# Attention scores as a 64-row and a 32-row product, queries copied earlier and moved once a period

## The chip, the cores and the metric

The kernel runs on one core of one Trainium2 chip. The metric is device time in microseconds (us) of one execution; the kernel before takes 558.39 us, the median of 3 runs (557.83 to 560.25). TensorE multiplies matrices (PE in the profile, its weight loads PEld), VectorE is DVE, ScalarE is ACT, GpSimd is POOL, and SyncE (SP) issues most of the DMAs.

## The reference

One layer in four parts, on x of 16 sequences, 128 steps, 128 features:

```
h   = LSTM(x, h0 = cond)                      # 128 steps in sequence
lat = h @ Wkv_down                            # 32 latents per position
k,v = lat @ Wk_up, lat @ Wv_up                # 16 heads of 64
y   = causal_softmax(q k^T / 8) v @ Wout,  q = h @ Wq
x1  = x + y
g   = GRU(x1, h0 = cond), every 4th state also through tanh(g @ Wp + bp)
out = x1 + sum over the 2 best of 8 experts: gate_e * (gelu(g @ w1_e + b1_e) @ w2_e + b2_e)
```

The kernel folds Wq and Wk_up into one matrix, so that a score is a product over 32 latents: score(head, t, s) = q'(head, t) · lat(s), with q' of 32 numbers for each head and position. Most values are carried as a high and a low part in 16-bit floats; a product of two such values is formed as high·high + high·low + low·high.

## The kernel before

The whole kernel is one pipeline of 154 steps, written out by hand: for each step k every engine has a fixed list of instructions, and semaphores order them across engines. In step k TensorE does step k of the LSTM (pL) and step k - 18 of the GRU (pG; LAG = 18); between the two recurrences the rest of the work is laid as filler. Engines issue in order, so an instruction that waits holds back everything behind it on its engine.

The rest goes in periods of 8 steps. At k = 8, 16, ... `lat_q` computes the latents (pY) and the queries q' (pC) of the last 8 positions of all 16 sequences. The queries lie in pC as 128 rows (4 heads of 32 latents) by 512 columns (4 groups of heads, 8 positions, 16 sequences). `q_copy` (ACT, in the same step) takes their high part into `qh`, `q_rest` (DVE, a step later) the low part. `spread_queries` (SP) then carries them by DMA into `qbd`, a block-diagonal form of 128 rows by 128 columns for each sequence: row block q holds only head q of each group, the rest is zeros. The latents stand four times one under the other in `lathi` and `latlo`, so the product over 128 rows sums only over the 32 latents of each head.

A period's scores are made in four units n (four sequences each) in steps with k mod 8 = 2, 3, 4, 5 (`scores`, the last work of TensorE in the step): one matmul that writes the mask (cmask), then for each sequence three products qh·lathi, qh·latlo, ql·lathi, each over 128 rows and with L = 8(p + 1) columns for period p = 0 to 15. Units alternate between the banks pH[0] and pS. A step after them follow the row maximum (`maximum`, DVE, mx) and the exponentials (`exps`, ACT), then in steps k mod 8 = 4 to 7 the transposes (`turn_probs`, pC<-ident,P) and in 5 to 8 the values.

Steps up to 30 (WARM_END) hold no expert work; there `keep_warm` issues matmuls on zeros (still, 128x512) so that TensorE has work. In the same steps the expert weights are prepared: `setup` on ACT and `setup_late` on DVE split w1 into w1hi and w1lo and b2 into the parts of b2P. From step 30 on the experts' matmuls (pH<-ghi,w1hi and the like; pY, pC, pV<-w,hid) fill TensorE. In steps 3 to 6 the weights are folded by matmuls over 64 rows, in single precision (pH<-hid, 64*128 and 64*32 in the profile).

Of the kernel before, what the change touches and what calls it, by code (L numbers as in the profile page):

```python
# [8 lines left out]
GS = 8  # L9
# [14 lines left out]
W1_STEP = (17, 18, 19, 20, 21, 22, 23, 25)  # L24
# [117 lines left out]
def build(nc, a, out):  # L142
# [8 lines left out]
    with ctx:  # L151
# [77 lines left out]
        qh = sb("qh", [128, 2, B, 2, HG, TB], f16)  # L229
        qbd = sb("qbd", [128, 2, 4, 2, HQ, 32], f16)  # L230
# [48 lines left out]
        loaded_b2 = sem("loaded_b2")  # L279
        loaded_moe = sem("loaded_moe")  # L280
# [50 lines left out]
        qbd_done = [sem(f"qbd_done{n}") for n in range(2)]  # L331
# [33 lines left out]
        NCLEAR = 12  # L365
# [17 lines left out]
        def _(sp):  # L383
# [16 lines left out]
            for t, name in ((w1, "w1"), (tri, "tri"), (b1, "b1"), (w2, "w2")):  # L400
                sp.dma_start(whole(t), a[name]).then_inc(loaded_moe, 16)

            def spread_queries(n):
                p, u = divmod(n, NU)
                if u == 0:
                    sp.wait_ge(q_lo, p + 1)
                if n == 0:
                    sp.wait_ge(cleared, NCLEAR)
                if n >= 2:
                    sp.wait_ge(s_mm, n - 1)  # L410
                for q in range(HQ):
                    r = slice(32 * q, 32 * q + 32)
                    sp.dma_start(qbd[r, n % 2, :, :, q, :].rearrange("p j l c -> p (j l) c"),
                                 qh[r, p % 2, 4 * u:4 * u + 4, :, :, :].rearrange("p b l g t -> p (b l) (g t)")).then_inc(qbd_done[n % 2], 16)
# [7 lines left out]
            for k in range(STEPS + 2):  # L422
                n = unit_at(k, O_S)
                if unit_at(k + 1, O_S) is not None and (n is None or n + 1 != unit_at(k + 1, O_S)):
                    spread_queries(unit_at(k + 1, O_S))
                if unit_at(k + 2, O_S) is not None and unit_at(k + 1, O_S) is not None:
                    spread_queries(unit_at(k + 2, O_S))
# [11 lines left out]
        def _(pool):  # L439
# [6 lines left out]
            pool.memset(whole(qbd), 0.0).then_inc(cleared, 1)  # L446
# [8 lines left out]
            assert NCLEAR == 12  # L455
# [30 lines left out]
        def _(pe):  # L486
# [62 lines left out]
            def scores(n, k):  # L549
# [5 lines left out]
                pe.wait_ge(qbd_done[n % 2], 16 * HQ * (n // 2 + 1))  # L555
# [155 lines left out]
            for k in range(STEPS):  # L711
# [8 lines left out]
                if unit_at(k, O_T) is not None:  # L720
                    turn_probs(unit_at(k, O_T), k)
# [45 lines left out]
                if k < WARM_END:  # L767
# [7 lines left out]
        def _(act):  # L775
# [19 lines left out]
            def setup(k):  # L795
# [10 lines left out]
                if k == 9:  # L806
                    act.wait_ge(loaded_gru, 4 * 16)
                    A(gW1[:, :, :], gWh[:, :, :], ACT.Copy, scale=0.5 * SP).then_inc(set_gru, 1)
                if k == 10:
# [9 lines left out]
                if k in (26, 27):  # L819
                    c = slice(512 * (k - 26), 512 * (k - 25))  # L820
                    act.wait_ge(loaded_b2, 3 * 16)
                    A(b2P[:, c], b2[:, c], ACT.Copy).then_inc(set_b2, 1)
                if k in (28, 29):
                    c = slice(512 * (k - 28), 512 * (k - 27))
                    act.wait_ge(set_b2lo, k - 27)
                    A(b2P[64:128, c], b2[64:128, c], ACT.Copy).then_inc(set_b2, 1)
                if k in (30, 31):
                    c = slice(512 * (k - 30), 512 * (k - 29))
                    act.wait_ge(set_b2lo, k - 27)
                    A(b2P[96:128, c], b2[96:128, c], ACT.Copy).then_inc(set_b2, 1)  # L830
                if k in W1_STEP:
                    e = W1_STEP.index(k)
                    act.wait_ge(loaded_moe, 4 * 16)
# [5 lines left out]
            def q_copy(p):  # L839
                act.wait_ge(q_mm, p + 1)  # L840
                if p >= 2:
                    for half in range(2):
                        act.wait_ge(qbd_done[half], 16 * HQ * NU // 2 * (p - 1))
                A(qh[:, p % 2, :, 0, :, :], pC[:, :].rearrange("p (g s b) -> p b g s", g=HG, b=B),
# [18 lines left out]
            def activate(m, e, half, chunks):  # L863
                n = UP_NO[(m, e, half)]
                act.wait_ge(up_mm, n + 1)
                if n == 0:
                    act.wait_ge(loaded_moe, 4 * 16)
# [7 lines left out]
            for k in range(STEPS):  # L875
# [43 lines left out]
                if latents_at(k) is not None:  # L919
# [7 lines left out]
        def _(dve):  # L927
# [50 lines left out]
            def q_rest(p):  # L978
                dve.wait_ge(q_hi, p + 1)
                V.scalar_tensor_tensor(qh[:, p % 2, :, 1, :, :],  # L980
                                       pC[:, :].rearrange("p (g s b) -> p b g s", g=HG, b=B), 1.0 / SP,
                                       qh[:, p % 2, :, 0, :, :], ALU.mult, ALU.subtract).then_inc(q_lo, 1)
# [127 lines left out]
            def setup_late(k):  # L1110
                if k in (27, 28):
# [129 lines left out]
```

## Time and profile before

| | |
|---|---|
| median of 3 runs | 558.39 us (557.83 to 560.25) |
| the profiled execution, its own time | 559.31 us |
| its span, first to last instruction | 557.4 us |
| TensorE busy | 521.5 us, 94% |
| VectorE busy | 420.2 us, 75% |
| ScalarE busy | 347.8 us, 62% |
| mean granted TensorE clock | 0.957 of 2.4 GHz |

A busy share is an average over stages; matmuls overlap, so the duration of one (some 0.17 to 0.2 us for the small ones) is far longer than the distance from its start to the next start, and the distance is what it costs TensorE. A merged row of the timeline gives the first start, the time to the last end and the count. Rows of the chain give only work on the path that ended last.

### The profile page before, as it was taken

The numbers are of one execution on the slowest core, as the hardware profiler recorded it, in microseconds if no ns is written. First come the engines' busy times: TensorE is split into PE (matmuls) and PEld (weight loads), VectorE is DVE, ScalarE is ACT, GpSimd is POOL, SyncE is SP. The second block draws the span as 40 slices with busy tenths as digits, with TensorE's granted clock in tenths as the row PEclk, the third lists the DMA queues.
The fourth block names the chain that finished last, engine by engine and source line by source line (L and its number), as shares of the span: only waits on it lengthen the run. The fifth ranks groups of instructions, "written<-read, shape, count | busy, mean of one in ns | idle before, by whom it ended". The sixth has DMA issues, their size and how long they took to land.

```text
span 557.4 us, 20232 instructions
## 1 busy us (share of the span) xinstructions
PE 521.5 (94%) x7376; PEld 480.1 (86%) x7418; DVE 420.2 (75%) x2338; ACT 347.8 (62%) x1297; POOL 32.2 (6%) x85
## 2 busy tenths in 40 slices
PE   8979888899789999999999999999999999989998
PEld 3746676789779999999999999999999998889997
DVE  4536787869877888888888888888989797864442
ACT  2224454677357676767676767776767767666662
POOL 7000000000000000000000000000000000000000
PEclk9689969799959999999999999999999999999999
DMA  8910101001010101010101010101101010100000
GB/s 211 351 11 11 16 6 14 11 7 16 13 15 5 19 3 21 13 20 3 21 14 19 4 19 15 17 8 13 15 15 15 8 15 15 18 2 1 13 6 11
DMA packets 75118, 14.32 MB, mean 26 GB/s; under 512 B 71411, under 2 KB 74111, under 8 KB 74638
## 3 DMA queue, kind: packets, MB, share of 16 engines
q1 hardware_dynamic: 74566, 11.96, 11.8%
q8 instruction: 60, 0.98, 0.8%
q10 hardware_dynamic: 456, 1.08, 0.6%
q14 instruction: 36, 0.29, 0.2%
HBM read 7.78 MB, written 1.05 MB: 16 GB/s over the span
## 4 chain that ended last, share of the span: by engine, by line
PE 75%; DVE 15%; ACT 4%; issue 4%; DMA 1%; SPq 1%; POOL 0%; ACTq 0%; DVEq 0%; POOLq 0%
PE pH L488 21%; PE pY L488 12%; PE pG L488 12%; PE pL L488 9%; PE pV L488 8%; PE pC L580 6%; PE pC L488 4%; PE pS L488 4%; DVE latNlo L990 2%; DVE mx L996 1%; DVE acc L1085 1%; ACT hid L872 1%; DVE ghi L1164 1%; DVE gB L1161 1%; DVE glo L1167 1%
## 5 line engine op out<-in xcount | busy, mean ns | idle before, releaser
L872 ACT ACTIVATE hid<-pH,b 128x256 f32<-128x256 f32 (+1 forms) x320 | 114.8, 438 | 4.9 <-PE pH L488 4.9
L488 PE MATMUL pY<-w,hid 128*128 128x128 f32 x608 | 84.2, 281 | 0.0
L488 PE MATMUL pH<-ghi,w1hi 128*128 128x256 f16 (+1 forms) x320 | 75.9, 253 | 3.1 <-ACT hid L872 1.6
L488 PE MATMUL pH<-glo,w1hi 128*128 128x256 f16 (+1 forms) x320 | 76.0, 254 | 0.0
L488 PE MATMUL pH<-ghi,w1lo 128*128 128x256 f16 (+1 forms) x320 | 75.9, 254 | 0.0
L488 PEld LDWEIGHTS pY<-w,hid 128*128 128x128 f32 x608 | 73.7, 191 | 0.2
L879 ACT ACTIVATE gT<-pG 128x32 f32<-128x32 f32 x128 | 24.6, 192 | 68.2 <-PE pG L488 68.2
L1139 DVE SCALAR_TENSOR_TENSOR gRZ<-gT,g 128x32 f32<-128x32 f32 x128 | 24.4, 190 | 39.2 <-ACT gT L879 37.9
L910 ACT ACTIVATE lC<-lT 128x16 f32<-128x16 f32 x128 | 28.0, 219 | 39.0 <-DVE lT L1176 38.7
L580 PE MATMUL pC<-ident,P 128*128 128x128 f32 x256 | 43.2, 294 | 6.4 <-DVE acc L1085 4.6
L897 ACT ACTIVATE lT<-pL 128x64 f32<-128x64 f32 x128 | 28.8, 225 | 32.1 <-PE pL L488 22.4
L861 ACT ACTIVATE PThi<-pC 128x512 f16<-128x512 f32 x64 | 38.1, 596 | 15.5 <-PE pC L580 15.4
L488 PEld LDWEIGHTS pL<-hhi,lWhi 128*128 128x128 f16 x512 | 42.5, 116 | 5.9 <-DVE hhi L1181 4.6
L488 PE MATMUL pG<-gRZ,gW 128*128 128x16 f32 x256 | 45.4, 253 | 2.4 <-DVE gRZ L1139 1.7
L488 PEld LDWEIGHTS pG<-gRZ,gW 128*128 128x128 f32 x256 | 40.5, 198 | 5.4 <-DVE gRZ L1139 4.3
L1002 DVE SCALAR_TENSOR_TENSOR PTlo<-pC,PThi 128x512 f16<-128x512 f32 x64 | 43.7, 682 | 0.5 <-ACT PThi L861 0.3
L488 PE MATMUL pL<-hhi,lWhi 128*128 128x16 f16 x512 | 41.3, 170 | 1.6 <-DVE hhi L1181 1.6
L488 PE MATMUL pL<-hhi,lWlo 128*128 128x16 f16 x512 | 41.1, 170 | 0.0
L1161 DVE TENSOR_TENSOR gB<-gRZ,gC 128x16 f32<-128x16 f32 x128 | 22.3, 174 | 24.6 <-ACT gC L894 23.1
L488 PEld LDWEIGHTS pH<-ghi,w1hi 128*128 128x128 f16 x320 | 32.8, 103 | 5.8 <-issue 2.1
L580 PEld LDWEIGHTS pC<-ident,P 128*128 128x128 f32 x256 | 30.2, 153 | 8.6 <-issue 6.0
L894 ACT ACTIVATE gC<-pG 128x16 f32<-128x16 f32 x128 | 23.9, 187 | 19.0 <-PE pG L488 18.9
(181 smaller groups left out, 1619.5 us busy)
## 6 DMA issues: line engine op xcount, KB each, us to landing
w<-in_w SPq DMA_DIRECT2D x2, 2048.0 KB, 13.0
qbd<-qh SPq DMA_DIRECT2D x256, 16.0 KB, 1.9
out<-acc SPq DMA_DIRECT2D x16, 64.0 KB, 1.5
xT<-in_xT ACTq DMA_DIRECT2D x1, 960.0 KB, 7.7
hid<-in_WqT SPq DMA_DIRECT2D x1, 512.0 KB, 5.3
hid<-in_Wout SPq DMA_DIRECT2D x1, 512.0 KB, 9.9
lWh<-in_lWh SPq DMA_DIRECT2D x1, 256.0 KB, 2.8
lWx<-in_lWx SPq DMA_DIRECT2D x1, 256.0 KB, 3.1
```

What stands on the lines that cost most here:

```text
L488: return nc.tensor.matmul(o, lhsT=lhsT, rhs=rhs, start=start, stop=stop, skip_group_check=True)
L580: last = nc.tensor.transpose(pC[:, 128 * j:128 * (j + 1)], P[:, n % 2, j, :], ident[:, :])
L861: A(PThi[:, n % 2, :, :].rearrange("p j q -> p (j q)"), pC[:, :], ACT.Copy, scale=SH).then_inc(pt_done, 1)
L872: A(hid[:, e % NHID, c, 0:W], pH[half][:, W * at:W * (at + 1)], ACT.Gelu, bias=b1[:, e, c:c + 1], scale=1.0 / SP).then_inc(gelu, 1)
L879: A(gT[:, :, :], pG[:, 0:2, g % GS, :], ACT.Tanh, scale=1.0 / SP).then_inc(g_tanh, 1)
L894: A(gC[:, :], pG[:, 2, g % GS, :], ACT.Tanh, scale=1.0 / SP).then_inc(g_c, 1)
L897: A(lT[:, 0:4, :], pL[:, :, t % GS, :], ACT.Tanh, scale=1.0 / SP).then_inc(l_tanh, 1)
L910: A(lC[:, :], lT[:, 4, :], ACT.Tanh, scale=0.5).then_inc(l_tc, 1)
L990: V.transpose(turned[rows, :, 0:LD], whole_t[rows, :, 32 * j:32 * j + 32]).then_inc(latn_done, 1)
L1002: V.scalar_tensor_tensor(PTlo[:, n % 2, :, :].rearrange("p j q -> p (j q)"), pC[:, :], SH, PThi[:, n % 2, :, :].rearrange("p j q -> p (j q ...
L1139: V.scalar_tensor_tensor(gRZ[:, :, :], gT[:, :, :], 1.0, g8[:, at:last + 1:last - at, :], ALU.add, ALU.mult).then_inc(g_rh, 1)
L1161: V.tensor_tensor(gB[:, :], gRZ[:, 1, :], gC[:, :], ALU.mult).then_inc(g_b, 1)
```

## The change

Scores. The block-diagonal `qbd` is replaced by `qst`, 64 rows by 128 columns for each sequence: rows 0 to 31 hold the high parts of all 16 heads, rows 32 to 63 the low parts. Since the latents' high part stands in rows 0 to 31 and again in 32 to 63, one product over 64 rows gives qh·lathi + ql·lathi, and one over 32 rows gives qh·latlo. A unit is the mask matmul and eight products in place of twelve, and a unit alternates 64-row and 32-row products.

Queries. `q_copy` stands directly behind the LSTM's tanh in its step instead of at the step's end (from step 18 on). `spread_queries` is called once a period and issues 8 DMAs of 32 KB, four as soon as the high parts are there and four for the low parts, in place of 16 DMAs of 16 KB in four groups. The clearing of qbd on POOL is gone.

Weights. The splits of w1 and b2 and two of the GRU's scalings stand in other steps: b2 in 9 to 17 and one ACT part in 25 (before: 26 to 31), w1's low parts in 18, 19 (two), 24 (two), 26 (two) and 27 (before: 18 to 24 and 26). w1 has a semaphore of its own. `keep_warm` gets two matmuls ahead of `turn_probs` in steps 18 to 29, and loses two in step 23.

```diff
+W1_HI = {17: (0,), 18: (1,), 19: (2, 3), 24: (4,), 25: (5,), 26: (6,), 27: (7,)}
+W1_LO = {18: (0,), 19: (1, 2), 24: (3, 4), 26: (5, 6), 27: (7,)}
+B2_LO = {10: (64, 0), 11: (64, 1), 12: (96, 0), 17: (96, 1)}
...
-            def spread_queries(n):
-                p, u = divmod(n, NU)
-                if u == 0:
-                    sp.wait_ge(q_lo, p + 1)
...
-                if n >= 2:
-                    sp.wait_ge(s_mm, n - 1)
-                for q in range(HQ):
-                    r = slice(32 * q, 32 * q + 32)
-                    sp.dma_start(qbd[r, n % 2, :, :, q, :].rearrange("p j l c -> p (j l) c"),
...
+            def spread_queries(p):
+                for r, (l, ready) in enumerate(((0, q_hi), (1, q_lo))):
+                    sp.wait_ge(ready, p + 1)
+                    if p >= 2 and r == 0:
+                        sp.wait_ge(s_mm, NU * (p - 1))
+                    for q in range(HQ):
+                        sp.dma_start(qst[LD * r:LD * (r + 1), p % 2, :, 32 * q:32 * q + 32],
+                                     qh[32 * q:32 * q + 32, p % 2, l, :, :, :].rearrange("p b g t -> p b (g t)")).then_inc(qst_done[p % 2], 16)
...
-                pe.wait_ge(qbd_done[n % 2], 16 * HQ * (n // 2 + 1))
+                pe.wait_ge(qst_done[p % 2], 16 * 2 * HQ * (p // 2 + 1))
...
-                    S = S4[:, j, :]
-                    mm(S, flat(qbd[:, n % 2, j, 0, :, :]), lathi[:, b, 0:L])
-                    mm(S, flat(qbd[:, n % 2, j, 0, :, :]), latlo[:, b, 0:L])
-                    last = mm(S, flat(qbd[:, n % 2, j, 1, :, :]), lathi[:, b, 0:L])
+                    mm(S4[:, j, :], qst[:, p % 2, b, :], lathi[0:2 * LD, b, 0:L])
+                    last = mm(S4[:, j, :], qst[0:LD, p % 2, b, :], latlo[0:LD, b, 0:L])
...
                 if unit_at(k, O_T) is not None:
+                    if LAG <= k < WARM_END:
+                        keep_warm(k, 2)
                     turn_probs(unit_at(k, O_T), k)
...
-                if k < WARM_END:
+                if k < WARM_END and not (LAG <= k and t % GS == GS - 1):
                     keep_warm(k, startup_fill(k))
...
+                if latents_at(k) is not None and k >= LAG:
+                    q_copy(latents_at(k))
                 if unit_at(k, O_T) is not None and not early and k >= LAG:
...
-                if latents_at(k) is not None:
+                if latents_at(k) is not None and k < LAG:
                     q_copy(latents_at(k))
```

On TensorE a unit of period 9 (L = 80, step 82) stands so before the change, from the transpose ahead of it to the GRU's next step:

```order
L659 MATMUL pV<-ident,x1T 128x128
L488 MATMUL pH<-cmask,ident 128x4x8 [waits exp_done,gelu,qbd_done0,lat_split]
L488 MATMUL pH<-lathi,qbd 128x80
L488 MATMUL pH<-latlo,qbd 128x80
L488 MATMUL pH<-lathi,qbd 128x80 x2
L488 MATMUL pH<-latlo,qbd 128x80
L488 MATMUL pH<-lathi,qbd 128x80 x2
L488 MATMUL pH<-latlo,qbd 128x80
L488 MATMUL pH<-lathi,qbd 128x80 x2
L488 MATMUL pH<-latlo,qbd 128x80
L488 MATMUL pH<-lathi,qbd 128x80
L488 MATMUL pG<-ghi,gWhi 128x16 [waits g_hi]
```

and so after it (the size is that of the output; the products with lathi are over 64 rows, those with latlo over 32):

```order
L654 MATMUL pV<-ident,x1T 128x128
L485 MATMUL pH<-cmask,ident 128x4x8 [waits exp_done,gelu,qst_done1,lat_split]
L485 MATMUL pH<-lathi,qst 128x80
L485 MATMUL pH<-latlo,qst 128x80
L485 MATMUL pH<-lathi,qst 128x80
L485 MATMUL pH<-latlo,qst 128x80
L485 MATMUL pH<-lathi,qst 128x80
L485 MATMUL pH<-latlo,qst 128x80
L485 MATMUL pH<-lathi,qst 128x80
L485 MATMUL pH<-latlo,qst 128x80
L485 MATMUL pG<-ghi,gWhi 128x16 [waits g_hi]
```

Nothing else moves around a unit: four products are gone, and the GRU's matmuls follow directly behind the last 32-row product.

On ACT, in step 80 of the same period, the copy of the queries stands behind lC before the change:

```order
L894 ACTIVATE gC<-pG 128x16 [waits g_cand]
L897 ACTIVATE lT<-pL 128x64 [waits l_gates]
L910 ACTIVATE lC<-lT 128x16 [waits l_c]
L844 ACTIVATE qh<-pC 128x16x32 [waits qbd_done1,qbd_done0,q_mm]
L879 ACTIVATE gT<-pG 128x32 [waits g_rz]
```

and ahead of it after the change:

```order
L885 ACTIVATE gC<-pG 128x16 [waits g_cand]
L888 ACTIVATE lT<-pL 128x64 [waits l_gates]
L835 ACTIVATE qh<-pC 128x512 [waits qst_done0,q_mm]
L903 ACTIVATE lC<-lT 128x16 [waits l_c]
L870 ACTIVATE gT<-pG 128x32 [waits g_rz]
```

The copy has moved past lC, the second tanh of the LSTM step.

On DVE the split of w1 stands in step 20 ahead of the row maximum before the change:

```order
L1139 SCALAR_TENSOR_TENSOR gRZ<-gT,g 128x32 [waits g_tanh]
L1141 SCALAR_TENSOR_TENSOR gA<-gT,g 128x16
L1122 SCALAR_TENSOR_TENSOR w1lo<-w,w1hi 128x512 [waits set_w1hi]
L996 TENSOR_REDUCE mx<-pS 128x4 [waits exp_done,s_mm]
L1002 SCALAR_TENSOR_TENSOR PTlo<-pC,PThi 128x512 [waits o_mm,pt_done]
```

and the same place after it:

```order
L1127 SCALAR_TENSOR_TENSOR gRZ<-gT,g 128x32 [waits g_tanh]
L1129 SCALAR_TENSOR_TENSOR gA<-gT,g 128x16
L988 TENSOR_REDUCE mx<-pS 128x4 [waits exp_done,s_mm]
L994 SCALAR_TENSOR_TENSOR PTlo<-pC,PThi 128x512 [waits o_mm,pt_done]
```

The split has left this step.

## Rows read from the trace of the kernel before

**Rows 1.** The page, its first lines: span, and busy time of the engines.

```profile
span 557.4 us, 20232 instructions
...
PE 521.5 (94%) x7376; PEld 480.1 (86%) x7418; DVE 420.2 (75%) x2338; ACT 347.8 (62%) x1297; POOL 32.2 (6%) x85
```

**Rows 2.** The page, the chain that ended last: shares of the span by engine.

```profile
PE 75%; DVE 15%; ACT 4%; issue 4%; DMA 1%; SPq 1%; POOL 0%; ACTq 0%; DVEq 0%; POOLq 0%
```

**Rows 3.** The chain in period 9: start us, us, what (12 or 13 score matmuls).

```profile
299.99 0.44 PE pH L488 x12
...
307.41 0.46 PE pH L488 x13
...
310.44 0.46 PE pS L488 x13
```

**Rows 4.** The chain in periods 0, 1, 3 and 15: units of 13 score matmuls.

```profile
41.81 0.33 PE pS L488 x13
...
73.99 0.33 PE pS L488 x13
...
131.14 0.32 PE pS L488 x13
...
476.21 0.69 PE pH L488 x13
```

**Rows 5.** Timeline of PE behind the second unit of period 9: start us, us, what.

```profile
303.49 0.17 PE L488 MATMUL pG<-ghi,gWlo 128*128 128x16 f16 x1
303.67 0.21 PE L488 MATMUL pG<-glo,gWhi 128*128 128x16 f16 x2
304.33 0.63 PE L580 MATMUL pC<-ident,P 128*128 128x128 f32 x4 [0.46 <-DVE acc L1085]
```

**Rows 6.** Timeline of PE where 128-row and 64-row matmuls meet (steps 3 and 4).

```profile
17.68 0.50 PE L488 MATMUL pH<-hid 64*128 64x32 f32 x3
18.11 0.18 PE L488 MATMUL pL<-hhi,lWhi 128*128 128x16 f16 x1
18.15 0.17 PE L488 MATMUL pL<-hhi,lWlo 128*128 128x16 f16 x1
...
18.32 0.24 PE L488 MATMUL pL<-hlo,lWhi 128*128 128x16 f16 x4
18.50 0.41 PE L488 MATMUL pH<-hid 64*128 64x32 f32 x2
```

**Rows 7.** Timeline of PE where both neighbours have 128 rows (step 85).

```profile
308.60 0.18 PE L488 MATMUL pV<-latNhi,PTlo 128*128 128x33 f16 x1
308.63 0.37 PE L488 MATMUL pG<-gRZ,gW 128*128 128x16 f32 x2
308.85 0.17 PE L488 MATMUL pL<-hhi,lWhi 128*128 128x16 f16 x1
308.87 0.17 PE L488 MATMUL pL<-hhi,lWlo 128*128 128x16 f16 x1
```

**Rows 8.** The chain in steps 19 and 28: the splits on DVE.

```profile
65.65 0.60 DVE w1lo L1122
...
99.51 0.69 DVE b L1114
```

**Rows 9.** Timeline of ACT and DVE around the copy of the queries, step 80.

```profile
292.77 0.22 ACT L910 ACTIVATE lC<-lT 128x16 f32<-128x16 f32 x1 [0.93 <-DVE lT L1176]
292.89 0.58 ACT L844 ACTIVATE qh<-pC 128x512 f16<-128x512 f32 x1
...
293.79 0.68 DVE L980 SCALAR_TENSOR_TENSOR qh<-pC,qh 128x512 f16<-128x512 f32 x1
```

**Rows 10.** All instructions on tile qbd: the DMAs, min/median/max ns and landing.

```profile
L413 SPq DMA_DIRECT2D qbd<-qh x256: 585/611/1947, 34.7 to 482.2; - x128
...
DMA to landing us min/median/max: 1.9/1.9/3.8
```

**Rows 11.** Busy time by stage: span, PE, PEld, DVE, ACT, POOL, PE clock, DMA.

```profile
154.00:181.00 27.00, 24.75 (x345) 22.43 (x348) 21.20 (x127) 17.08 (x67) 1.42 (x4) 0.71 0.09 10
181.00:474.00 293.00, 285.93 (x4339) 277.24 (x4356) 251.41 (x1431) 208.23 (x758) 13.87 (x40) 1.00 0.11 14
```

More of the change, by code:

```diff
@@ L330, in build @@
         q_lo = sem("q_lo")
-        qbd_done = [sem(f"qbd_done{n}") for n in range(2)]
+        qst_done = [sem(f"qst_done{n}") for n in range(2)]
         s_mm = sem("s_mm")
@@ L364, in build @@
         HALVES = (0.5, 1.0)
-        NCLEAR = 12
+        NCLEAR = 11
         PARTS = (0, 64, 96)
@@ L399, in _ @@
                 sp.dma_start(b2[q:q + 1, :], a["b2"].rearrange("(o e) d -> o (e d)", o=1)).then_inc(loaded_b2, 16)
[L400 removed]
+            sp.dma_start(whole(w1), a["w1"]).then_inc(loaded_w1, 16)
+            for t, name in ((tri, "tri"), (b1, "b1"), (w2, "w2")):
                 sp.dma_start(whole(t), a[name]).then_inc(loaded_moe, 16)
[L403 to L414 removed]
+            def spread_queries(p):
[6 more added lines that the diff above has]
+                                     qh[32 * q:32 * q + 32, p % 2, l, :, :, :].rearrange("p b g t -> p b (g t)")).then_inc(qst_done[p % 2], 16)
             def store(i):
@@ L422, in _ @@
             for k in range(STEPS + 2):
[L423 to L427, printed above, removed]
+                if latents_at(k - 1) is not None:
+                    spread_queries(latents_at(k - 1))
                 for i in range(NG):
@@ L818, in setup @@
                     A(gWhi[:, :, :], gW2[:, 0:2, :], ACT.Copy).then_inc(set_gru, 1)
[L819 to L833, printed above, removed]
+                if k in B2_HI:
+                    q, half = B2_HI[k]
+                    c = slice(512 * half, 512 * (half + 1))
+                    if q == 0:
+                        act.wait_ge(loaded_b2, 3 * 16)
+                    else:
+                        act.wait_ge(set_b2lo, PARTS[1:].index(q) * 2 + half + 1)
+                    A(b2P[q:128, c], b2[q:128, c], ACT.Copy).then_inc(set_b2, 1)
+                for e in W1_HI.get(k, ()):
+                    act.wait_ge(loaded_w1, 16)
                     A(w1hi[:, e, :], w1[:, e, :], ACT.Copy, scale=SW).then_inc(set_w1hi, 1)
@@ L841, in q_copy @@
                 if p >= 2:
-                    for half in range(2):
-                        act.wait_ge(qbd_done[half], 16 * HQ * NU // 2 * (p - 1))
-                A(qh[:, p % 2, :, 0, :, :], pC[:, :].rearrange("p (g s b) -> p b g s", g=HG, b=B),
+                    act.wait_ge(qst_done[p % 2], 16 * 2 * HQ * (p // 2))
+                A(qh[:, p % 2, 0, :, :, :], pC[:, :].rearrange("p (g s b) -> p b g s", g=HG, b=B),
                   ACT.Copy, scale=1.0 / SP).then_inc(q_hi, 1)
@@ L1110, in setup_late @@
             def setup_late(k):
-                if k in (27, 28):
-                    c = slice(512 * (k - 27), 512 * (k - 26))
-                    dve.wait_ge(set_b2, k - 26)
-                    V.tensor_tensor(b2[64:128, c], b2[64:128, c], b2P[64:128, c], ALU.subtract).then_inc(set_b2lo, 1)
-                if k in (29, 30):
-                    c = slice(512 * (k - 29), 512 * (k - 28))
-                    dve.wait_ge(set_b2, k - 26)
-                    V.tensor_tensor(b2[96:128, c], b2[96:128, c], b2P[96:128, c], ALU.subtract).then_inc(set_b2lo, 1)
-                if k - 1 in W1_STEP:
-                    e = W1_STEP.index(k - 1)
+                if k in B2_LO:
+                    q, half = B2_LO[k]
+                    c = slice(512 * half, 512 * (half + 1))
+                    dve.wait_ge(set_b2, (PARTS.index(q) - 1) * 2 + half + 1)
+                    V.tensor_tensor(b2[q:128, c], b2[q:128, c], b2P[q:128, c], ALU.subtract).then_inc(set_b2lo, 1)
+                for e in W1_LO.get(k, ()):
                     dve.wait_ge(set_w1hi, e + 1)
```

21 lines of the change are left out of this document (10 added, 11 removed).

## The prediction

> **What bounds the kernel now.** I read the busy times first, then the chain that ended last, then the timeline at the units of scores. TensorE is busy 521.5 of 557.4 us and VectorE 420.2 [rows 1]; the chain is 75% TensorE's [rows 2]. By stages, from 181 to 474 us TensorE is busy 285.9 of 293 us at full clock [rows 11]: there nearly every nanosecond added to TensorE's list lengthens the run, and nearly every one taken away shortens it.
>
> A unit of scores is worth its place on the chain. In period 9 the first, third and fourth unit stand on it with 0.44 to 0.46 us each [rows 3]. The second does not: behind it TensorE waits for VectorE, from 303.49 to 303.67 for glo and then 0.46 us for the accumulation [rows 5], some 0.64 us in all. So three units of four pay, and the second has 0.6 us of cover. The chain shows the same in periods 5 to 14. In period 3 all four units are on it, in period 0 all four, in period 1 one, in period 2 two, in period 15 two [rows 4] (one unit of each of periods 0, 1, 3 and 15 is shown); period 4 ran partly at the low clock and I count two.
>
> **What the change removes.** A unit is 13 matmuls in 0.32, 0.46 and 0.69 us at L = 32, 80 and 128 [rows 3, 4], so 0.025, 0.035 and 0.053 us a matmul. Four of 13 go: 0.10, 0.14 and 0.21 us. I take a product over 64 or 32 rows to stream like one over 128: in the fold the single-precision matmuls over 64 rows stand (0.50 - 0.27)/2 = 0.11 us apart, and with 128 rows two stand 0.37 - 0.26 = 0.11 us apart [rows 6, 7] (0.27 and 0.26 us is one's own duration). By this term alone the change would save 4/13 of the units' time.
>
> **What it adds: changes of the number of rows.** In the trace before TensorE goes from 128 rows to 64 and back only at the fold. From the last matmul over 128 rows (18.32 + 0.24 - 0.17 = 18.39) to the second over 64 rows (18.50 + 0.41 - 0.27 = 18.64) pass 0.25 us [rows 6]; between the same kinds at 128 rows, from 308.60 to 308.63 + 0.37 - 0.26 = 308.74, 0.14 us [rows 7]. The way in costs 0.10 us. On the way out the last fold matmul starts at 17.68 + 0.50 - 0.27 = 17.91 and the second LSTM matmul at 18.15, 0.24 us [rows 6]; at 128 rows 308.74 to 308.87, 0.13 us [rows 7]. The way out costs 0.11 us. In both places the next weights are loaded only once the array is empty, though nothing in the program holds them.
>
> The new unit goes 128, 64, 32, 64, 32, 64, 32, 64, 32, 128: nine changes. Two of them (128 to 64, and back to 128) have the price just read, though from fp32 neighbours; seven are between 64 and 32, of which this trace shows none. Bounds for one of those: 0, if only leaving the full array costs, and 0.11, the dearest change seen. I take 0.095 for all nine: nearest is the only kind of row change there is to read (0.10 and 0.11), a little less because 16-bit weights load faster than the fp32 ones of those rows.
>
> The Trainium skill, "TensorEngine Tiling (Array Packing)", Key Properties, says that a change of the tiling mode, not just of the tile, drains the engine, and lists 64 and 32 rows as different modes. By that rule all nine changes cost, and the sum is the one below. The trace agrees for 128 to 64 and back (0.10 and 0.11 us); it does not show 64 to 32.
>
> **The unit after.** Nine of the 13 matmuls stay and 9 x 0.095 = 0.855 us is added: 0.22 + 0.855 = 1.08 us at L = 32 (+0.76), 0.32 + 0.855 = 1.17 at L = 80 (+0.71), 0.48 + 0.855 = 1.34 at L = 128 (+0.64). The uncovered second unit of a period grows by 0.7 against 0.64 us of waiting behind it: about nothing.
>
> **The sum of the units.** Periods 3 to 15: 4 + 2 + 10 x 3 + 2 = 38 units on the chain, at 0.71 on average: 27.0 us; less 0.7, since in periods 5 to 8 the first unit runs side by side with a chain on VectorE with some 0.2 us between them. Periods 0 to 2: 4 + 1 + 2 = 7 units at 0.76: 5.3 us. Together **+31.6 us**.
>
> **The queries.** In step 80 the low part is ready at 293.79 + 0.68 = 294.47 [rows 9]; four DMAs are issued at 0.61 us each and the last lands 1.9 us later [rows 10], at 298.8, and the unit runs at about 299.9 [rows 3]. Now all 8 DMAs must be in before the first unit. The first four go with the high part, whose copy moves up: ScalarE sat idle 0.93 us ahead of lC [rows 9], the copy takes 0.58, so it fits and lC does not move. They leave SP's queue at about 292.4 + 2.4 = 294.9, the low ones follow until 297.3 and land at 299.2, 0.7 us ahead of the unit. What waits behind the copy on ScalarE is lC alone, and the copy waits for nothing there, since pC is complete before the LSTM's matmuls of the step. Bounds: nothing, and with the longest landing seen, 3.8 us [rows 10], 1.2 us late in a period. I take 0, by the median landing. SP has only the stores behind these DMAs, and in period 0 TensorE waits for the queries before and after alike. That 128 fewer DMAs are issued saves nothing: the others are hidden.
>
> **The weights and keep_warm.** On VectorE the splits were on the chain in steps 19 to 21 (0.60 each) and 27 to 29 (0.69 each) [rows 8], where one of each stands. New: two in 19, none in 20 and 21, one in 27, none in 28 and 29: 0.6 + 1.4 = 2.0 us off. The longer units stand in the same steps and take up about half: -1.0. The 12 added keep_warm matmuls less 2 are 0.215 us each (512 columns at the pace of rows 4's 0.053 us for 128): 2.2 us, of which about half where VectorE is not later: +1.0. I take 0 for both, bounds -2 and +2. The parts of b2 in steps 9 to 17 (0.6 to 0.7 us each on two engines) lie beside the zeros' matmuls.
>
> **Total.** 559.3 us is the time of the profiled execution; it is 0.9 above the median of 558.4, so the forecast is made on the median: 558.4 + 31.6 = **590 us**. Its own range: price of a change 0.08 to 0.11 (-6, +6), cover +-3, queries up to +4: 580 to 601.
>
> **The rivals.**
> - *Only leaving and entering the full array costs.* For: that is all the trace shows. Two changes at 0.105 = 0.21 us less 0.10 to 0.21: +0.11 at L = 32, +0.07 at 80, 0 at 128. Over 45 units: +3. With the weights 558 to 564, at **561 us**. Every 0.01 us that an inner change costs adds 45 x 7 x 0.01 = 3 us, so from 0.01 us on it is slower for certain.
> - *Nothing drains with 16-bit operands*, so it gets faster: the fold's price would belong to fp32. Against: the last matmul in front of the fold is 16-bit, and it is there that the weights wait. Then 38 x 0.14 + 7 x 0.10 = 6.0 us off, and the weights' 1.0: **552 us**. It turns at 0.14/9 = 0.016 us a change.
> - *A change between 64 and 32 rows costs part*, 0.03 to 0.06 us: 45 x 7 x 0.045 = 14 on top of 561: **575 us**.
> - *The clock.* From 154 to 181 us the mean granted clock was 0.71 [rows 11], 58% of 27 us at 1.2 GHz; if all of it scaled this cost 27 x 0.58/2 = 7.8 us. An array that is empty for most of 1.1 us in a unit may be granted less. One more such stretch: **598 us**. Against: at full clock from 181 on TensorE stayed there with waits of 0.6 us in each period.
>
> **Chances.** All nine drain: 0.60. Full array only: 0.18. Part: 0.08. Nothing drains: 0.08. The clock on top of the first: 0.06. Eight in ten reach from 557 to 602. A measurement of this kernel can tell about 0.5% from no change, 2.8 us. Faster by more: the whole of "nothing drains" and 0.02 of "full array only", 0.10. Within it: 0.10. Slower: the rest, 0.80.
>
> **What would show it.** Right: the timeline of a unit shows distances of 0.12 to 0.13 us between its products, each weight load starting about 0.1 us behind the matmul ahead of it; a unit of period 9 takes 1.1 to 1.2 us, and a period 2 us more. Wrong: products 0.035 us apart (nothing drains), or a gap only at the unit's two ends; or weight loads of the score matmuls waiting for a DMA (queries late); or a lower clock beyond 181 us.

## The result, and the profile after

The changed kernel takes 606.4 us (604.7 to 612.4, 4 runs) against 558.1 us (557.4 to 560.3, now 4 runs) for the kernel before: a ratio of 1.087, 95% interval 1.083 to 1.090. It is 48.3 us slower, where 31.6 were forecast, and the time lies above the range of 580 to 601 us.

The page of the profile of the changed kernel: span, busy times and the chain's shares by engine:

```profile
span 606.2 us, 19610 instructions
...
PE 576.4 (95%) x7131; PEld 506.9 (84%) x7172; DVE 422.3 (70%) x2338; ACT 350.4 (58%) x1297; POOL 30.6 (5%) x84
...
PE 87%; DVE 5%; ACT 3%; issue 3%; SPq 1%; DMA 0%; ACTq 0%; POOL 0%; DVEq 0%; POOLq 0%
```

The span grew by 48.8 us [rows 1] with 245 matmuls fewer, and TensorE's share of the chain from 75% [rows 2] to 87%; VectorE's fell from 15% to 5%. TensorE is "busy" 55 us longer although it does less: a product's record lasts 0.20 to 0.21 us and the next one starts 0.14 us behind it, so the records cover the time in which the next one is held back.

The timeline of TensorE at the first unit of scores in period 9 (start us, us, what), and under it its weight loads:

```profile
323.97 0.18 PE L485 MATMUL pH<-cmask,ident 128*128 128x32 bf16 x1
324.08 0.21 PE L485 MATMUL pH<-lathi,qst 64*128 64x80 f16 x1
324.22 0.20 PE L485 MATMUL pH<-latlo,qst 32*128 32x80 f16 x1
324.36 0.21 PE L485 MATMUL pH<-lathi,qst 64*128 64x80 f16 x1
...
325.05 0.20 PE L485 MATMUL pH<-latlo,qst 32*128 32x80 f16 x1
325.19 0.18 PE L485 MATMUL pG<-ghi,gWhi 128*128 128x16 f16 x1
```

```profile
323.83 0.13 PEld L485 LDWEIGHTS pH<-cmask,ident 128*128 128x128 bf16 x1
324.08 0.09 PEld L485 LDWEIGHTS pH<-lathi,qst 64*128 64x128 f16 x1
324.22 0.09 PEld L485 LDWEIGHTS pH<-latlo,qst 32*128 32x128 f16 x1
```

The products stand 0.14 us apart, where one of 80 columns needs 0.035, and each weight load starts only 0.11 to 0.14 us behind the matmul ahead of it (323.97, 324.08, 324.22), not under it as at full rows. Each of the nine changes of rows costs some 0.10 us, those between 64 and 32 rows like those from and to 128. The unit takes 325.19 - 323.97 = 1.22 us, where the chain had 0.46 [rows 3].

The chain in period 9:

```profile
324.13 1.12 PE pH L485 x9
...
327.96 1.12 PE pS L485 x9
...
332.34 1.12 PE pH L485 x9
...
336.15 1.13 PE pS L485 x9
```

All four units are on it now. Behind the second one TensorE no longer waits for VectorE; the 0.46 us of [rows 5] are used up:

```profile
329.12 0.20 PE L485 MATMUL pG<-glo,gWhi 128*128 128x16 f16 x2
329.27 0.63 PE L575 MATMUL pC<-ident,P 128*128 128x128 f32 x4
```

Busy time by stage of the changed kernel: window, its length, PE, PEld, DVE, ACT and POOL busy, mean granted clock, DMA share, GB/s:

```profile
185.00:224.00 39.00, 38.84 (x540) 36.59 (x542) 31.72 (x184) 25.71 (x96) 2.10 (x6) 1.00 0.11 13
224.00:259.00 35.00, 34.46 (x429) 31.85 (x431) 25.49 (x147) 21.13 (x78) 1.39 (x4) 0.90 0.11 15
259.00:417.00 158.00, 156.77 (x2104) 144.35 (x2113) 126.43 (x723) 104.79 (x382) 6.95 (x20) 1.00 0.10 12
417.00:450.00 33.00, 32.57 (x415) 29.29 (x416) 25.16 (x143) 20.86 (x75) 1.39 (x4) 0.95 0.08 12
450.00:515.00 65.00, 63.20 (x815) 56.60 (x818) 50.05 (x278) 42.25 (x150) 2.77 (x8) 1.00 0.10 13
515.00:552.00 37.00, 34.90 (x305) 29.65 (x305) 20.89 (x102) 18.87 (x59) 0.64 (x2) 0.82 0.03 4
```

Before, the granted clock was 1.00 from 181 to 474 us [rows 11] and on to the end of the run. Now it drops, in four stretches in the three windows with a mean below 1.00 (two of them in the last), to 1.2 GHz for some 24 us together (35 x 0.10, 33 x 0.05 and 37 x 0.18 us, each doubled, since a window wholly at 1.2 GHz would show 0.50). Each begins between the first unit of a period and 2 us behind its last one.

The queries, by SyncE's queue in steps 80 and 88, the first unit behind the second of these, and all instructions on the tile qst:

```profile
316.56 5.30 SPq L414 DMA_DIRECT2D qst<-qh  x8
...
347.92 6.22 SPq L414 DMA_DIRECT2D qst<-qh  x8
```

```profile
355.91 0.18 PE L485 MATMUL pH<-cmask,ident 128*128 128x32 bf16 x1 [0.41 <-issue]
```

```profile
L414 SPq DMA_DIRECT2D qst<-qh x128: 585/629/1553, 32.0 to 515.3; - x128
...
DMA to landing us min/median/max: 2.1/2.1/3.5
```

The landing is counted from the start of the issue, and the last of the eight takes longer than the median. In step 80 it is this one (its row in the timeline of SyncE and its group of DMA issues, us to landing):

```profile
321.22 0.63 SPq L414 DMA_DIRECT2D qst<-qh  x1
qst<-qh SPq DMA_DIRECT2D x1, 32.0 KB, 2.3
```

It lands at 321.22 + 2.3 = 323.5; the unit starts at 323.97, some 0.45 us later and without a wait. In step 88 one issue took 1.5 us and the eight 0.9 us longer; from the start of the matmul ahead to that of the unit pass 0.72 us, where 0.14 is usual. Such waits stand in periods 6, 8, 10 and 12 to 15, by 3.9 us in all over the usual 0.14. In periods 6 and 14 no issue was long; there the last transfers landed 3.2 to 3.3 us after the start of their issue.

Two sums of whole periods from this trace and that before, by the starts of gT's tanh eight steps apart: period 9 takes 31.36 us (before 29.07), as forecast 2.1 to 2.3 more. Periods 6, 12 and 15, in which the clock dropped, take 34.3, 33.8 and 36.8 us (before 29.2, 29.6, 28.9), 5.1, 4.2 and 7.9 more. These three alone grow by 17.2 us, where the forecast had some 5. So 12 us of the shortfall, which is 16.7 us by the medians, lie in them.

### The profile page after: what moved, and what is told of

It is laid out like the page before. It is cut to its first block, busy times and chain, and to the rows that moved or that the text cites. A ratio compares the mean times of both kernels' runs of the same rounds, so it can differ in the third digit from the quotient of the medians.

```text
span 606.2 us, 19610 instructions
## 1 busy us (share of the span) xinstructions
PE 576.4 (95%) x7131; PEld 506.9 (84%) x7172; DVE 422.3 (70%) x2338; ACT 350.4 (58%) x1297; POOL 30.6 (5%) x84
## 4 chain that ended last, share of the span: by engine, by line
PE 87%; DVE 5%; ACT 3%; issue 3%; SPq 1%; DMA 0%; ACTq 0%; POOL 0%; DVEq 0%; POOLq 0%
PE pH L485 25%; PE pY L485 14%; PE pG L485 13%; PE pL L485 8%; PE pS L485 8%; PE pV L485 8%; PE pC L575 6%; PE pC L485 6%; ACT hid L863 1%; SPq L414 1%; ACT PThi L852 1%; PE pV L654 0%; DMA qst<-qh 0%; DVE oK L1159 0%; DVE w1lo L1110 0%
## 5 line engine op out<-in xcount | busy, mean ns | idle before, releaser
L485 PE MATMUL pY<-w,hid 128*128 128x128 f32 x608 | 87.9, 289 | 0.0
L485 PEld LDWEIGHTS pY<-w,hid 128*128 128x128 f32 x608 | 77.0, 199 | 0.3
L903 ACT ACTIVATE lC<-lT 128x16 f32<-128x16 f32 x128 | 28.0, 219 | 33.4 <-DVE lT L1164 33.1
L575 PE MATMUL pC<-ident,P 128*128 128x128 f32 x256 | 45.2, 305 | 1.0 <-DVE PTlo L994 0.9
L1149 DVE TENSOR_TENSOR gB<-gRZ,gC 128x16 f32<-128x16 f32 x128 | 22.4, 175 | 30.9 <-ACT gC L885 29.6
L485 PE MATMUL pH<-still 128*128 128x512 bf16 x109 | 35.4, 422 | 1.5 <-issue 0.8
```

The lines of the kernel that those rows point to most:

```text
L485: return nc.tensor.matmul(o, lhsT=lhsT, rhs=rhs, start=start, stop=stop, skip_group_check=True)
L575: last = nc.tensor.transpose(pC[:, 128 * j:128 * (j + 1)], P[:, n % 2, j, :], ident[:, :])
L903: A(lC[:, :], lT[:, 4, :], ACT.Tanh, scale=0.5).then_inc(l_tc, 1)
L1149: V.tensor_tensor(gB[:, :], gRZ[:, 1, :], gC[:, :], ALU.mult).then_inc(g_b, 1)
```

## The experiments

Two theories stood at first. A: each of the nine changes of rows holds the next weight load until the array is empty, 0.10 us, and the rest of the excess is the clock's, which falls because of it (A2). B: the excess has to do with the two products and their late queries, whatever their rows. The ratio given with each run is to the kernel before, timed on the same chip.

**Fewer changes of rows.** The same products in another order, four over 64 rows and then four over 32: three changes in a unit.

```
-                    mm(S4[:, j, :], qst[:, p % 2, b, :], lathi[0:2 * LD, b, 0:L])
-                    last = mm(S4[:, j, :], qst[0:LD, p % 2, b, :], latlo[0:LD, b, 0:L])
+                    mm(S4[:, j, :], qst[:, p % 2, b, :], lathi[0:2 * LD, b, 0:L])
+                for j in range(4):
+                    b = 4 * u + j
+                    last = mm(S4[:, j, :], qst[0:LD, p % 2, b, :], latlo[0:LD, b, 0:L])
```

> The changed kernel, but a unit makes its four 64-row products first and then its four 32-row ones: the number of rows changes 3 times in a unit instead of 9, and no product is left out. If every change of rows costs 0.10 us (theory A, from the distances of 0.139 us between products of 80 columns in the changed kernel), a unit falls from 1.22 to about 0.60 us at L = 80, and the time by 45 units x 0.62 = 28 us, to 578 us; if the clock falls in the changed kernel because the array stands empty (theory A2), up to 8 us more, 570 us. If the time went into the later queries, the weights' new steps or into products over few rows as such (theory B), it stays at 600 us or above.

Measured: 569.9 us, ratio 1.021 (1.017 to 1.025). The timeline of a unit of period 9:

```profile
304.75 0.18 PE L485 MATMUL pH<-cmask,ident 128*128 128x32 bf16 x1
304.86 0.31 PE L485 MATMUL pH<-lathi,qst 64*128 64x80 f16 x4
305.10 0.31 PE L485 MATMUL pH<-latlo,qst 32*128 32x80 f16 x4
305.35 0.18 PE L485 MATMUL pG<-ghi,gWhi 128*128 128x16 f16 x1
```

0.60 us instead of 1.22. Six changes fewer give back 36.5 us: B is out, and the time is that of A2. With three changes the clock still drops, but less, in period 15 alone: its mean is 1.00 from 185 to 480 us and 0.91 from 480 to 520 us.

**Two changes.** Both products over 64 rows; the low latents meet the low queries too, which adds their product to the scores.

```
-                    last = mm(S4[:, j, :], qst[0:LD, p % 2, b, :], latlo[0:LD, b, 0:L])
+                    last = mm(S4[:, j, :], qst[:, p % 2, b, :], latlo[0:2 * LD, b, 0:L])
```

> The changed kernel, but the product with latlo runs over the same 64 rows as the one with lathi (it then also adds low queries times low latents). Two changes of rows in a unit instead of 9, both against the full array. Theory A: a unit at L = 80 takes about 0.50 us, the time falls by 45 x 0.72 = 32 us to 574 us, with the clock's share 566. If a change between 64 and 32 rows were cheap and only leaving the full array dear, it would stay near 600 us. Theory B: no change from 606.

Measured: 563.4 us, ratio 1.011 (1.007 to 1.014), granted clock 0.970 in the mean. The unit of period 9:

```profile
299.61 0.18 PE L485 MATMUL pH<-cmask,ident 128*128 128x32 bf16 x1
299.72 0.21 PE L485 MATMUL pH<-lathi,qst 64*128 64x80 f16 x1
299.76 0.20 PE L485 MATMUL pH<-latlo,qst 64*128 64x80 f16 x1
...
300.11 0.18 PE L485 MATMUL pG<-ghi,gWhi 128*128 128x16 f16 x1
```

Products over 64 rows stand 0.035 to 0.04 us apart, as those over 128 do. It isn't the small number of rows that costs, but the change of it; nor do 64 rows lower the clock, which stays at 1.00 from 175 to 555 us. The time is 2.6 us below the lower of theory A's two (566).

**No change.** qst gets 128 rows with zeros in the lower half, and both products run over 128.

```
-        qst = sb("qst", [2 * LD, 2, B, H * TB], f16)
+        qst = sb("qst", [128, 2, B, H * TB], f16)
...
+                    mm(S4[:, j, :], qst[:, p % 2, b, :], lathi[:, b, 0:L])
+                    last = mm(S4[:, j, :], qst[:, p % 2, b, :], latlo[:, b, 0:L])
```

> The changed kernel with the lower 64 rows of qst filled with zeros, both products over 128 rows: no change of rows anywhere in a unit, still eight products (the second adds low queries times low latents). Theory A: a unit at L = 80 takes 0.32 us and the time falls to about 558 to 564 us; whatever it lies above the kernel before less 6 us (four matmuls fewer) is the price of the later queries. With the clock back at 0.957 it is the lower end. Theory B: no change from 606.

Measured: 556.35 us, ratio 0.996 (0.994 to 0.998). The unit of period 9:

```profile
297.48 0.18 PE L488 MATMUL pH<-cmask,ident 128*128 128x32 bf16 x1
297.51 0.20 PE L488 MATMUL pH<-lathi,qst 128*128 128x80 f16 x1
...
297.79 0.17 PE L488 MATMUL pG<-ghi,gWhi 128*128 128x16 f16 x1
```

0.31 us; the time is 1.7 us below the expected range, and the clock stays at 1.00 from 175 to 550 us. By the number of changes in a unit, 0, 2, 3 and 9, the units take 0.31, 0.50, 0.60 and 1.22 us: 0.095, 0.097 and 0.101 us a change. The times go 556, 563, 570 and 606.

**The rest alone.** The kernel before with everything of the change but the scores and their transfers: splits of the weights, keep_warm, and the sooner copy of the queries.

```
+                if latents_at(k) is not None and k >= LAG:
+                    q_copy(latents_at(k))
...
+W1_HI = {17: (0,), 18: (1,), 19: (2, 3), 24: (4,), 25: (5,), 26: (6,), 27: (7,)}
```

> The kernel before with all of the change but the scores and the queries' DMAs: block-diagonal queries, twelve products over 128 rows, 16 DMAs a period; the queries' copy early, the weights in their new steps, keep_warm as changed. Theory A: the time of the kernel before, 558 us, within 2 us. Theory B (the time went into these parts): 570 us or more.

Measured: 555.75 us, ratio 0.995 (0.992 to 0.997): 2.9 us come from here. Against it the version with 128 rows is 0.6 us slower, which the spread of the runs doesn't tell from equal, although it has four products fewer in a unit. Something takes their gain; that is asked below.

**Length or emptiness.** To tell the time of the drains from what they do to the clock, the version with 128 rows gets nine products with a tile of zeros in each unit, 240 columns each: the length of a change, but with the array full.

```
+                bank = (pS if n % 2 else pH[0])[:, 0:240]
+                mm(bank, still[:, 0:128], still[:, 0:240], start=True)
                 mm(S4[:, :, L - TB:L], ident16[:, :], cmask[:, :, :], start=True)
                 for j in range(4):
+                    mm(bank, still[:, 0:128], still[:, 0:240])
                     mm(S4[:, j, :], qst[:, p % 2, b, :], lathi[:, b, 0:L])
+                    mm(bank, still[:, 0:128], still[:, 0:240])
```

> The queries' products over 128 rows as in the run before (one shape in the whole unit, 554.1 us span, clock 0.966), and in each unit of scores nine products of a zero weight tile with 240 columns, over all 128 rows, one ahead of each product. They last 0.10 us each, as long as a change of rows, and add zeros, so a unit should be as long as the changed kernel's (1.2 us at 80 keys), with the array at work and not idle. Theory 'the drain lowers the clock too': the units cost the same 2.3 to 2.7 us per period as in the changed kernel, some 43 us in all, but the further low stretches of the clock after 181 us do not come; clock 0.96 or more, time 594 to 600. Rival 'only the length of the units counts, and the low stretches come with longer units, however they are filled': 603 to 609, clock 0.94. Third case: the filling is hidden by waits that the drains did not use, under 590.

Measured: 599.9 us, ratio 1.075 (1.072 to 1.078). The unit of period 9, and busy time in the same stages as those of the changed kernel (its units there start 1 to 6 us sooner):

```profile
321.31 0.26 PE L488 MATMUL pH<-still 128*128 128x240 bf16 x1 [0.49 <-issue]
...
321.44 0.26 PE L488 MATMUL pH<-still 128*128 128x240 bf16 x1
321.55 0.20 PE L488 MATMUL pH<-lathi,qst 128*128 128x80 f16 x1
...
322.55 0.17 PE L488 MATMUL pG<-ghi,gWhi 128*128 128x16 f16 x1
```

```profile
224.00:259.00 35.00, 34.32 (x506) 33.12 (x505) 27.36 (x161) 22.26 (x82) 1.39 (x4) 1.00 0.11 16
...
417.00:450.00 33.00, 32.10 (x461) 30.99 (x462) 25.85 (x148) 21.18 (x76) 1.38 (x4) 1.00 0.10 14
...
515.00:550.00 35.00, 33.08 (x399) 31.15 (x398) 21.56 (x106) 21.08 (x69) 0.89 (x3) 1.00 0.01 2
```

The unit is 322.55 - 321.31 = 1.24 us, as long as the changed kernel's 1.22. But the clock stays at 1.00 in all three stages, the mean over the span is 0.983 (changed kernel 0.938), and the kernel is 6.6 us faster. The length of nine changes is worth 599.9 - 556.35 = 43.5 us; that the array is empty in them, the other 6.6. The split is rough. By the starts of gT's tanh, periods 6, 12 and 15, where the changed kernel has its low stretches, take 104.9 us in it and 96.0 with the filling, so the low clock costs 8.9 us there; part of that is hidden in the medians, because the filled kernel waits longer for its queries (6.4 us over the usual 0.14 in periods 5 to 15, against 3.9 in the changed kernel and 4.1 with 128 rows). Those waits do not lower the clock by themselves, for here it stays at 1.00.

**The copy put back.** The version with 128 rows, with the copy of the queries at the end of its step again, 1.2 us later.

```
-                if latents_at(k) is not None and k >= LAG:
-                    q_copy(latents_at(k))
...
-                if latents_at(k) is not None and k < LAG:
+                if latents_at(k) is not None:
                     q_copy(latents_at(k))
```

> The version with 128 rows (556.35 us), with the copy of the queries put back behind the tanh of the cell at the end of the step, some 1.2 us later, so that all eight transfers start 1.2 us later. Theory 'the first unit of a period stands right at the landing of the eighth transfer': all of the 1.2 us shows at nearly every period of 4 to 15, 11 to 14 us in all, 567 to 570. Rival 'the transfers are hidden, as the prediction had it': 556 to 558. The gap ahead of the first unit should grow from 0.14 to 1.3 us in the periods where it is now 0.14.

Measured: 569.0 us, ratio 1.020 (1.017 to 1.024), 12.7 us slower than with the sooner copy. TensorE at the first unit of period 9:

```profile
303.24 0.31 PE L657 MATMUL pV<-ident,x1T 128*128 128x128 f32 x1
304.13 0.18 PE L488 MATMUL pH<-cmask,ident 128*128 128x32 bf16 x1 [0.58 <-issue]
```

0.89 us from start to start, 0.14 before, where 1.3 was expected: of some 1.2 us of delay 0.75 show here, since the last transfer had landed 0.4 us ahead of this unit; in periods in which TensorE waited already, more shows. The time is in the range of the theory all the same, and the rival "hidden" is out: eight transfers on one queue have little to spare, 0.4 us here. The sooner copy is what makes the two products possible without a loss.

**Two queues.** The version with 128 rows, with the low parts issued by GpSimd.

```
+                for q in range(HQ):
+                    pool.dma_start(qst[LD:2 * LD, p % 2, :, 32 * q:32 * q + 32],
+                                   qh[32 * q:32 * q + 32, p % 2, 1, :, :, :].rearrange("p b g t -> p b (g t)")).then_inc(qst_low[p % 2], 16)
```

> The version with 128 rows (556.35 us), with the four transfers of the low parts issued by GpSimd on its own queue, beside the four of the high parts on SyncE's. Theory 'the pitch of the eight issues on one queue makes the first unit late by 0.2 to 1.0 us in seven of twelve periods': those 4 to 5 us come back, 551 to 553. Rival 'an issue on GpSimd's queue takes longer than on SyncE's (over 1.3 us each), so that the low parts land later than now': slower than 556.35, up to 575. Third: the gain is taken by a wait elsewhere, 555 to 557.

Measured: 555.0 us, ratio 0.994 (0.992 to 0.996). SyncE's queue and GpSimd's in step 88, and the groups of DMA issues on the page of the profile (xcount, KB each, us to landing):

```profile
320.12 2.60 SPq L416 DMA_DIRECT2D qst<-qh  x4
```

```profile
322.77 2.60 POOL L476 DMA_DIRECT2D qst<-qh  x4 [3.32 <-issue]
```

```profile
qst<-qh SPq DMA_DIRECT2D x64, 32.0 KB, 2.1
qst<-qh POOLq DMA_DIRECT2D x64, 32.0 KB, 2.3
```

An issue on GpSimd costs the same 0.65 us, but nobody waits behind it, and the waits ahead of the first units are gone in periods 5 to 11 and 13. From step 18 to step 138 the kernel is 2.7 us shorter than with one queue; up to step 18 it is 2.4 us longer, and the sum is the third case of the expectation. The gain in the loop comes again in both later traces with two queues. The loss is seen in one trace, and kernels with the same instructions up to step 18 differ there by up to 1.5 us (63.3 and 64.2 us in two traces of the next kernel, 64.8 with one queue).

**Two queues from period 4 on.** As above, with SyncE issuing all eight in periods 0 to 3 (timed once more below); and the same transfers in the changed kernel, with its 64 and 32 rows.

```
+        ONE_Q = 4
...
-                for r, (l, ready) in enumerate(((0, q_hi), (1, q_lo))):
+                for r, (l, ready) in enumerate(((0, q_hi), (1, q_lo))[:2 if p < ONE_Q else 1]):
...
+                if p < ONE_Q:
+                    return
```

> The version with 128 rows and two queues, but in periods 0 to 3 all eight transfers are SyncE's again, and only from period 4 on GpSimd issues the low parts. In the run with two queues throughout, the loop was 2.7 us shorter than with one queue, and the part up to step 18 was 2.4 us longer. Theory 'GpSimd's issues are in the way of its own work only in the start-up, and from period 4 on they save the waits': both gains, 556.35 less 2.5 to 3.5, so 552.5 to 554. Rival 'the start-up was longer for another reason' : 555.

Measured: 555.1 us, ratio 0.994 (0.992 to 0.997), at the rival's 555 and above the 552.5 to 554 of the theory. Up to step 18 the trace had the time of one queue again (63.3 us; 64.8 with one queue, 67.2 with two), but the median doesn't tell this run from the one before, so it isn't shown that the start-up pays for the second queue.

> The changed kernel (606.4 us, 64 and 32 rows, nine changes of rows in a unit), with the low parts issued by GpSimd from period 4 on. In the changed kernel TensorE stands 0.4 to 0.75 us longer ahead of the first unit in seven periods, 4 us in all. Theory 'these waits are a term of their own beside the drains': 4 us back, 602. Rival 'the low stretches of the clock in steps with scores are set off by these waits (three of the four begin in a period with one)': the stretches go as well, clock 0.96 or more, 592 to 596. Rival 'the drains alone set off the stretches': they stay, clock 0.94, 601 to 604.

Measured: 600.2 us, ratio 1.076 (1.072 to 1.079): 6.3 us less than the changed kernel. Busy time by stage:

```profile
258.00:400.00 142.00, 142.00 (x1889) 129.73 (x1889) 115.03 (x647) 94.16 (x344) 16.72 (x34) 0.99 0.09 11
400.00:515.00 115.00, 113.53 (x1446) 102.19 (x1445) 88.61 (x491) 74.72 (x259) 15.38 (x30) 0.97 0.11 14
515.00:550.00 35.00, 33.33 (x347) 29.13 (x347) 20.84 (x102) 20.51 (x67) 0.65 (x2) 0.95 0.01 2
```

Of the 3.9 us of waits for the queries 1.1 are left, 2.8 us given back. Behind 258 us there are still four low stretches, but shorter ones, some 14 us together and not 24, and the mean clock is 0.949 and not 0.938. Two of them, at 397 and 431 us, begin in periods whose first unit did not wait at all. So none of the three expectations holds whole: the drains alone bring low stretches on, and with fewer waits there is less of them; whether the waits themselves add to them isn't shown by one pair of kernels.

**Where the 3 us of the rest come from.** The kernel before with the weights and keep_warm of the change, the copy at its old place.

```
-W1_STEP = (17, 18, 19, 20, 21, 22, 23, 25)
+W1_HI = {17: (0,), 18: (1,), 19: (2, 3), 24: (4,), 25: (5,), 26: (6,), 27: (7,)}
```

> The kernel before with the weights' splits in their new order and the moved keep_warm products, and nothing else (the copy of the queries at the end of its step, the old transfers and the three products). Theory 'the 3 us of the rest of the change come from the weights' splits, in steps 26 to 41': 555 to 556.5, and the part of steps 26 to 41 some 2.9 us shorter. Rival 'they come from the sooner copy of the queries': 557.5 to 559.

Measured: 557.2 us, ratio 0.996 (0.993 to 0.998), 2.2 us under the kernel before as it ran beside it (559.4): between the two expectations, and by the ratios (0.996 and 0.995) not to be told from the 2.9, so the sooner copy adds nothing clear. Steps 26 to 33 take 29.2 us (before 33.1), steps 34 to 41 27.2 both times: the gain is where the parts of b2 stood on VectorE's side of the chain [rows 8]. But the trace before also has a mean clock of 0.90 there, from 92 to 125 us, and this one 1.00; how much of the 3.8 us is the splits' and how much the clock's stays open.

> The version with 128 rows and two queues from period 4 on, timed again in five rounds beside the one above. Theory 'two products over 128 rows save 0.14 to 0.22 us in each unit on the chain, and with the queries in time this shows': 553 to 555, 1 to 3 us under the version with the weights alone. Rival 'what the products save is waited for elsewhere': the same as the weights alone within 1 us.

Measured beside it: 553.8 us, ratio 0.990 (0.987 to 0.993), 3.4 us under the weights alone. The same kernel had 0.994 in its first timing, so two products without a change of rows, with the queries in time, gain 0.6 to 1% on the kernel before. The loop shows it without the start-up: periods 5 to 15, at full clock in these traces, take 321.2 us with the rest alone, 320.6 with 128 rows and one queue, and 317.5, 317.5 and 318.0 in the three traces with two queues.

## Why the prediction was wrong

**The direction and the mechanism were right.** The unit is built as forecast: nine changes, each with a late weight load, 64 to 32 like 128 to 64. The Trainium skill, "TensorEngine Tiling (Array Packing)", Key Properties, has a drain at every change of the tiling mode; the runs with 0, 2, 3 and 9 changes agree and give its price, 0.10 us. "Only leaving the full array", "part" and "nothing drains" are out. (In the text the way in from 128 rows costs 0.10 us; its own numbers give 0.25 - 0.14 = 0.11, which changes nothing.)

**The sum was mis-sized**, and the ladder of kernels says where:

| Term | Forecast, us | Measured, us | From |
|---|---|---|---|
| nine changes, their length | +38.5 (45 units x 9 x 0.095) | +43.5 | 128 rows, empty against filled |
| clock | 0 (a rival of 0.06) | +6.6 (8.9 in periods 6, 12 and 15) | filled against changed kernel |
| four products fewer, and the queries | -6.9 | +0.6 | rest alone against 128 rows |
| weights, keep_warm, sooner copy | 0 | -2.9 | rest alone |
| sum | +31.6 | +47.8 | |

(-6.9 is the 38 x 0.145 + 7 x 0.10 + 0.7 that the forecast took off. Between the sum of 47.8 and the measured 48.3 lies the kernel before, 558.1 us beside the changed kernel and 558.6 beside the runs.) The first row is less wrong than it looks. In the eight periods from 5 to 14 without a low stretch the changed kernel takes 2.6 us more than the version with 128 rows, and the forecast had 3 x 0.855 = 2.6. Of the 5.0 us between 43.5 and 38.5, 2.3 are the longer waits for the queries in the filled kernel; the rest isn't accounted for.

**The step "The clock" failed: it was put at 0, and cost 6.6 to 8.9 us.** Nor does the range of 580 to 601 hold anything for it. The text had the mechanism, "An array that is empty for most of 1.1 us in a unit may be granted less", and its price, but weighed it with 0.06, since "at full clock from 181 on TensorE stayed there with waits of 0.6 us in each period". Those waits come once in a period; the drains are nine in a unit and four units in a period, and then the granted clock did fall, in four stretches. So the rival's mechanism came out, and even its 598 us, with one more low stretch, was too low. Filling the same time kept it at 1.00. The Trainium skill, "TensorE: Matmul & The Clock Gate", A second HAM failure mode: psum-queue depth-cycling, describes a clock that goes down and up because the engine idles shortly but often between its groups of matmuls, there through the cycling of PSUM banks; with another cause of the idle times, this pair of runs agrees (0.938 with empty stretches, 0.983 with filled ones). Between the stretches the clock stood at 1.00 in the same kernel with the same units; what picks the moment at which it falls isn't settled.

**The step "The queries" failed too, though not at its median.** Forecast: the last transfer lands "0.7 us ahead of the unit". In period 9 it lands 0.45 us ahead, and 7.0 us after the end of the copy, where the forecast had 6.8. That this is so near is in part luck, since two errors nearly cancel: the forecast added the landing to the end of the last issue, while the trace counts it from the start, 0.61 us too much; and the eight issues stand 0.665 us apart and not 0.61, and the last one lands after 2.3 us and not 1.9. What failed is to take 0 "by the median landing": all eight transfers must be in, with 0.45 us to spare, and in seven periods slower issues (up to 1.55 us) or landings (up to 3.5 us) made the unit late, 3.9 us in all. The bound of 1.2 us late per period was in the text; the value taken was the lower end. This is the larger part of why four products fewer gave nothing by themselves: in periods 5 to 15 they save 0.6 us with one queue and 3.2 to 3.7 with two. By whole kernels the gain with two queues is 0.3 to 2.5 us over the rest alone (ratios 0.994 and 0.990 against 0.995), and 3.4 over the weights alone.

**The third row also holds a wait that the changed kernel doesn't have.** The fourth unit of a period is followed by a GRU matmul that needs ScalarE's g, and with 128 rows the unit has become shorter than that:

```profile
307.87 0.18 ACT L903 ACTIVATE g<-pG 128x16 f32<-128x16 f32 x1
308.11 0.62 PE L488 MATMUL pG<-g,gW 128*128 128x16 f32 x4
```

The unit starts at 307.68 and its last product at 307.95; g is ready at 308.05. So this unit takes 0.42 us in periods 3 to 13 and not 0.23 to 0.41, and saves nothing in the early ones. In the changed kernel the longer unit covers the wait.

**"The uncovered second unit ... about nothing"** was about right in size (0.76 - 0.64 = 0.12 us), although the unit is on the chain now. Period 9 was forecast 2.1 us longer and is 2.3.

**The weights** were priced at 0 with bounds of 2; they gave 2.2 to 2.9, measured without the longer units. The longer units were to take half of the gain away and keep_warm to add 1.0; neither was measured by itself.

Open: the terms were measured one on top of the other. In the changed kernel the two queues gave 6.3 us, 2.8 of them waits; how the other 3.5 divide between clock and the start-up wasn't tried. Each trace is one execution; that the clock differs between the kernels is borne out by all their runs (0.930 to 0.946 changed, 0.946 to 0.954 with two queues, 0.977 to 0.983 filled, 0.963 to 0.972 with 128 rows).

## What to carry to other kernels

Count how often neighbouring matmuls differ in the number of rows, not how many matmuls there are: four products fewer are worth 0.14 us in a unit here, nine changes cost 0.9. If a smaller product is wanted, fill it up with zeros to the rows of its neighbours, or put products of equal rows together. When short idle times are added to TensorE many times over, set a price on the clock as well, and before many transfers are packed ahead of one wait, look at when the last of them is issued (at one queue's pitch eight take 5.3 us) and count with a slow one and not with the median.

## What the runs showed of the hardware

- A change of rows costs 0.095 to 0.101 us with fp16 operands, whether 128 to 64, 64 to 32 or back.
- Products over 64 rows stream as fast as over 128, 0.035 to 0.04 us for 80 columns.
- With idle stretches of 0.1 us, nine in a unit of 1.2 to 1.4 us, the granted clock fell at times from 1.00, to a mean of 0.82 from 515 to 552 us, and stood at 1.00 between; the same time filled with products of zeros left it at 1.00 from 175 us on. With three such stretches in a unit it fell behind 175 us in the last period alone, with two not at all.
- An issue of such a transfer (32 KB) takes 0.63 us on SyncE and 0.65 on GpSimd, with single ones of up to 1.55 us on SyncE in the changed kernel; from the start of the issue to the landing pass 2.1 and 2.3 us in the median, and up to 3.5 us. With half of them on GpSimd's queue the loop was 2.7 us shorter.
